# In the first two groups ScalarE also makes the lower part of R, eight more scaled copies of tri a tile

## The chip, the cores and the metric

The kernel runs on 1 core of a Trainium2 chip. Its time is device microseconds, the median over runs. TensorE (PE in the rows) multiplies matrices, VectorE (DVE) and ScalarE (ACT) work elementwise, GpSimd (POOL) does some small things, and SyncE (SP) issues the transfers.

## The reference, cut to what matters

A Mamba-2 mixer with a residual and a layer norm, then a gated feed-forward layer on 4-bit weights, again with a residual and a layer norm. Input is (16, 256, 256). The change lies in the mixer's decay matrices inside a chunk:

```python
zxbcdt = u @ W_in                       # z, xBC, dt
xBC = silu(causal_conv4(xBC) + conv_b)  # x, B, C
dt = softplus(dt + dt_bias); A = -exp(A_log)
dA = A * dt                             # one number per token and head (8 heads)
L = exp(segsum(dA))                     # decay from token s to token l
y_diag = einsum('bclhn,bcshn,bhcls,bcshp->bclhp', C, B, L, x * dt)
y = (y_diag + y_off + D * x) * silu(z); y = rmsnorm(y) * norm_scale
h = layernorm(u + y @ W_out)
out = layernorm(h + (gelu(h @ Wg.T) * (h @ Wu.T)) @ Wd.T)
```

## The kernel before

The work is cut into groups of tokens, in tiles of 128. Group -1 (`FIRST`) has two tiles, groups 0 to 6 have four, group 7 (`LAST`) has two. Each engine runs its own instruction stream, written out by hand, and semaphores join them. The names of the steps and their order are in `SLOTS`: for a group, the mixer's steps (x, z, CB, R, D, XT, Y, g, S, op, ln) stand between the sixteen units of the feed-forward layer of the group before it (gate, up, GELU, down). Group -1 has no group before it, so beside its mixer, and in group 0 beside both, stands the preparation of the weights: `decode`, `value` and `rest` on VectorE, `upper` and `lower` on ScalarE, the products of L655 and L657 on TensorE, placed by the tables `DECODE`, `VALUE`, `UPPER`, `TAKE_OFF` and `LOWER`. Groups 1 to 5 are one loop whose group number is a register; -1, 0, 6 and 7 are written out with a plain number.

Products in fp32 are made from operands that are split into an upper part, rounded to the matrix format, and a lower part, the rest. The same holds for dA. For each tile i the step R makes R[:, h, :] = tri * dA[:, i, h] for the 8 heads, in two parts: ScalarE makes the upper one with eight scaled copies (L728), VectorE the lower one with one multiplication on 128x1024 elements (L935). Group -1 writes them to the tile of hT (`R_first`), the others to the tile of uT. Step D on TensorE (L552, L553) waits for both parts (`R_h`, `R_l`) and multiplies them with `after_r` into two banks, which gives the sums of dA between two tokens. ScalarE takes the exponential of them into `dec` (L738; in tile 1 of group -1 into `act_sb`), VectorE multiplies them with the masked C B product `cb` (L953), and TensorE multiplies the result with xdt in step Y (L573, for odd tiles also L583). Then VectorE forms y (L965, L1002, L969), multiplies it with the gate z (L972), ScalarE squares it (L749) and rounds it to g_hi (L754), VectorE adds the squares (L976, L978) and makes g_lo (L980), TensorE multiplies with W_out, and VectorE adds to h_sb (L987). The layer norm ends in L1029, and the transposes of F1 (L626) start the feed-forward layer.

On ScalarE a unit is in_hi (L760) and the GELU (L774), on VectorE in_lo (L1035) and the gated product (L1049), which frees the up bank. The exponentials and the GELU use different tables of ScalarE, so a table load stands at each change between them in the groups that have both.

`wait_R` holds R of tile i until the E or D bank before it was read, since R has one buffer for all tiles.

Of the kernel before, what the change touches and what calls it, by code (L numbers as in the profile page):

```python
# [6 lines left out]
ACT = mybir.ActivationFunctionType  # L7
# [63 lines left out]
def kind_of(g):  # L71

    return {FIRST: "first", LAST: "last"}.get(g, "full") if isinstance(g, int) else "full"


def tiles(g):

    return 4 if kind_of(g) == "full" else 2
# [13 lines left out]
def split_name(name):  # L92

    number = "".join(c for c in name if c.isdigit())
    return name.replace(number, "") if number else name, int(number or 0)
# [15 lines left out]
def wait(eng, signal, group, k):  # L111

    value = signal.at(group, k)
    if not isinstance(value, int) or value > 0:
        eng.wait_ge(signal.sem, value)


def mamba_ffn_kernel(nc, u, u_t, W_in, channels, dt_bias, A_log, W_out, ffn_w, ffn_s, out):
    BATCH, SEQ, DM = u.shape
    DI = W_out.shape[0]  # L120
    H = dt_bias.shape[0]
# [34 lines left out]
    def width(g):  # L156
        return P * tiles(g)
# [3 lines left out]
    with ExitStack() as ctx:  # L161
        def sb(name, shape, dt=F32):
            return ctx.enter_context(nc.sbuf_tensor(name, shape, dt))

        def sig(name, per, first=None, step=1):
            return Signal(ctx.enter_context(nc.semaphore(name)), per, first, step)
# [10 lines left out]
        tri = sb("tri", [P, P])  # L177
# [19 lines left out]
        dA_hi, dA_lo = sb("dA_hi", [P, NT, H], F32R), sb("dA_lo", [P, NT, H], F32R)  # L197
# [28 lines left out]
        def R_of(g):  # L226
            return R_first if kind_of(g) == "first" else (R_hi, R_lo)

        def dec_of(g, i):
            return dec_first if kind_of(g) == "first" and i else dec  # L230
# [41 lines left out]
        R_h, R_l, dec_ok, W_ok = sig("R_hi_done", 4, 2), sig("R_lo_done", 4, 2), sig("decay_ready", 8, 4), sig("W_ready", 4, 2)  # L272
# [20 lines left out]
        def bank(g, use):  # L293
            return MB[USES[kind_of(g)].index(use) % 4]
# [6 lines left out]
        def wait_ready(eng, use, g):  # L301
            if isinstance(g, int) and g < FIRST:
                return
            s, k = ready(g, use)
            wait(eng, s, g, k)
# [25 lines left out]
        def wait_R(eng, i, g):  # L331

            if i:
                wait_ready(eng, f"D{i - 1}b" if i % 2 else f"E{i // 2 - 1}", g)
            elif kind_of(g) != "first":
                wait_ready(eng, "z3", g)
            wait(eng, dA_ok, g, 1)

        def f32(ap):
            return ap.bitcast(F32)  # L340

        def by_block(ap):
            return ap.rearrange("p (j l) -> p j l", j=JT)

        def tile_of(x, i):

            return x[:, 0:JT, i * P:(i + 1) * P]
# [331 lines left out]
        def _(act):  # L679
            def tanh(n, g):  # L680
                c = CONV_ORDER[n]
                wait(act, conv, g, 3 * n + 3)

                wait_ready(act, f"S{tiles(g - 1) - 1}", g - 1)
                if n >= 2:
                    wait(act, xbc_ok, g, n - 1)
                nc.scalar.activation(y[:, n % 2, 0:width(g)], xbc[:, c, 0:width(g)], ACT.Tanh).then_inc(x_tanh.sem, 1)

            def mixer(name, g):
                kind, i = split_name(name)  # L690
                if kind == "uT":

                    wait_ready(act, f"E{tiles(g - 1) // 2 - 1}", g - 1)
                    wait(act, uT_in, g, 1)
                    for k in range(KT):
                        nc.scalar.activation(uT_hi[:, k, 0:width(g)], u32[:, k, 0:width(g)], ACT.Copy)\
                            .then_inc(uT_h.sem, 1)
                elif kind == "x":
                    n = CONV_ORDER.index(i)
                    wait_ready(act, f"x{i}", g)  # L700

                    wait(act, y_step, g - 1, D_ADDED[tiles(g - 1) - 1])
                    nc.scalar.activation(xbc[:, i, 0:width(g)], bank(g, f"x{i}")[:, 0:width(g)], ACT.Identity,  # L703
                                         bias=chan[:, 24 + i:25 + i],
                                         scale=chan[:, 18 + i:19 + i]).then_inc(conv0.sem, 1)
                    if n == 0:
                        wait(act, dt_step, g, 3)
                        nc.scalar.activation(dte[:, 0:H * tiles(g)], dte[:, 0:H * tiles(g)], ACT.Exp).then_inc(dt_exp.sem, 1)
                    for m in (() if n < 2 else (0, 1) if n == 2 else (n - 1,)):
                        tanh(m, g)  # L710
                elif kind == "z":
                    if i == 3:
                        tanh(CT - 1, g)
                    wait_ready(act, f"z{i}", g)
                    wait(act, g_l, g - 1, tiles(g - 1))
                    nc.scalar.activation(zs[:, i, 0:width(g)], bank(g, f"z{i}")[:, 0:width(g)], ACT.Tanh, scale=0.5)\
                        .then_inc(z_tanh.sem, 1)
                elif kind == "CB":
                    wait_ready(act, f"CB{i}", g)
                    if i:  # L720
                        wait_ready(act, "Yoff0", g)
                    else:
                        wait_ready(act, f"Yoff{tiles(g - 1) // 2 - 1}", g - 1)
                    nc.scalar.activation(cb[:, 1, :], bank(g, f"CB{i}")[:, P:2 * P], ACT.Copy).then_inc(cb_act.sem, 1)
                elif kind == "R":
                    wait_R(act, i, g)
                    for h in range(H):
                        ins = nc.scalar.activation(R_of(g)[0][:, h, :], tri[:, :], ACT.Copy,  # L728
                                                   scale=f32(dA_hi[:, i, h:h + 1]))
                    ins.then_inc(R_h.sem, 1)  # L730
                elif kind == "D":
                    if i == 0:
                        wait_ready(act, f"Y{tiles(g - 1) - 1}", g - 1)
                    elif kind_of(g) != "first":
                        wait_ready(act, f"Y{i - 1}", g)
                    for n, use in enumerate((f"D{i}a", f"D{i}b")):
                        wait_ready(act, use, g)
                        nc.scalar.activation(dec_of(g, i)[:, 4 * n:4 * n + 4, :],  # L738
                                             bank(g, use)[:, :].rearrange("p (h l) -> p h l", h=4),
                                             ACT.Exp).then_inc(dec_ok.sem, 1)  # L740
                    if i % 2:

                        if i > 2:
                            wait_ready(act, f"S{i - 2}", g)
                        wait_ready(act, f"E{i // 2}", g)
                        nc.scalar.activation(y[:, 1, :], bank(g, f"E{i // 2}")[:, :], ACT.Exp).then_inc(e_ok.sem, 1)
                elif kind == "g":
                    wait(act, y_step, g, Y_DONE[i])
                    nc.scalar.activation(by_block(y[:, i % 2, :]), tile_of(zs, i), ACT.Square).then_inc(squared.sem, 1)  # L749
                    if i:  # L750
                        wait_ready(act, f"op{i - 1}", g)
                    else:
                        wait_ready(act, f"op{tiles(g - 1) - 1}", g - 1)
                    nc.scalar.activation(g_hi[:, :, :], tile_of(zs, i), ACT.Copy).then_inc(g_h.sem, 1)  # L754
# [53 lines left out]
            act.wait_ge(consts.sem, 5)  # L808
            nc.scalar.activation(minus_i, ident[:, :], ACT.Copy, scale=-1.0).then_inc(crt.sem, 1)
            mixer("uT", FIRST)  # L810
            act.wait_ge(bc_in.sem, 16)
            nc.scalar.activation(win_hi[:, :, B0:DT0], bc_raw[:, :, 0:DT0 - B0], ACT.Copy).then_inc(win_top.sem, 1)
# [15 lines left out]
        def _(dve):  # L828
# [62 lines left out]
            def mixer(name, g):  # L891
                kind, i = split_name(name)
# [3 lines left out]
                elif kind == "x":  # L896
# [5 lines left out]
                    for d in (1, 2, 3):  # L902
                        c = (3 - d) * CT + i
                        ins = stt(acc[:, :, d:], src[:, :, 0:SEQ - d], chan[:, c:c + 1], acc[:, :, d:],  # L904
                                  ALU.mult, ALU.add)
# [22 lines left out]
                elif kind == "CB":  # L928
# [1 line left out]
                    wait(dve, cb_act, g, i + 1)  # L930
                    tt(cb[:, 0, :], bank(g, f"CB{i}")[:, 0:P], tri[:, :], ALU.mult)
                    tt(cb[:, 2, :], bank(g, f"CB{i}")[:, 2 * P:3 * P], tri[:, :], ALU.mult).then_inc(cb_ok.sem, 1)
                elif kind == "R":
                    wait_R(dve, i, g)
                    tt(R_of(g)[1], tri[:, :].unsqueeze(1).to_broadcast([P, H, P]),  # L935
                       f32(dA_lo[:, i, :]).unsqueeze(2).to_broadcast([P, H, P]), ALU.mult).then_inc(R_l.sem, 1)
# [312 lines left out]
```

## Time and profile before

| | |
|---|---|
| median of 3 runs | 955.6 us (955.42 to 955.68) |
| profiled execution | 955.01 us, span 953.3 us |
| TensorE busy | 892.7 us (94%) |
| VectorE busy | 704.9 us (74%) |
| ScalarE busy | 532.2 us (56%) |
| mean granted TensorE clock | 0.971 of full speed |
| group -1 | up to about 75 us |
| group 0's mixer | about 75 to 178 us |

The span is the time from the first to the last instruction of the profiled execution. In a timeline each row is an operation: start, duration, engine, line, what it writes and reads, and in brackets for how long the engine had been idle before it and whose result released it. "issue" in the place of a releaser means that the profile shows none. Several operations of one line in a row are merged, as x8. Durations of neighbours can overlap a little, since an operation starts before the one ahead has fully ended.

### The profile page before, as it was taken

The numbers are of one execution on the slowest core, as the hardware profiler recorded it, in microseconds if no ns is written. First come the engines' busy times: TensorE is split into PE (matmuls) and PEld (weight loads), VectorE is DVE, ScalarE is ACT, GpSimd is POOL, SyncE is SP. The second block draws the span as 40 slices with busy tenths as digits, with TensorE's granted clock in tenths as the row PEclk, the third lists the DMA queues.
The fourth block names the chain that finished last, engine by engine and source line by source line (L and its number), as shares of the span: only waits on it lengthen the run. The fifth ranks groups of instructions, "written<-read, shape, count | busy, mean of one in ns | idle before, by whom it ended". The sixth has DMA issues, their size and how long they took to land.

```text
span 953.3 us, 16507 instructions
## 1 busy us (share of the span) xinstructions
PE 892.7 (94%) x5632; PEld 773.0 (81%) x5632; DVE 704.9 (74%) x1566; ACT 532.2 (56%) x1016; POOL 72.3 (8%) x104
## 2 busy tenths in 40 slices
PE   4777789899999999999999999999999999999997
PEld 3446678788898888888888888888888888888887
DVE  6767988787769776786779876786779776867453
ACT  4743486448645775448735674547635674456232
POOL 2101000200011000200020000200020000200000
PEclk9787899999999999999999999999999999999999
DMA  4111100010002000010001000010002000100010
GB/s 135 33 58 49 32 18 12 23 45 1 1 23 67 0 0 22 22 44 0 0 22 66 0 0 22 31 35 0 0 22 67 1 1 13 45 12 1 1 35 12
DMA packets 18651, 23.13 MB, mean 24 GB/s; under 512 B 1584, under 2 KB 15152, under 8 KB 18608
## 3 DMA queue, kind: packets, MB, share of 16 engines
q1 hardware_dynamic: 18176, 22.56, 7.4%
q8 instruction: 24, 0.39, 0.2%
q14 instruction: 19, 0.16, 0.1%
q10 hardware_dynamic: 432, 0.03, 0.0%
HBM read 14.19 MB, written 4.19 MB: 19 GB/s over the span
## 4 chain that ended last, share of the span: by engine, by line
PE 78%; DVE 10%; issue 6%; POOL 3%; ACT 2%; DMA 1%; POOLq 0%; DVEq 0%; SPq 0%; ACTq 0%
PE gate_bank L493 6%; PE up_bank L493 6%; PE up_bank L495 6%; PE up_bank L494 6%; PE gate_bank L495 5%; PE gate_bank L494 5%; PE down L493 5%; PE down L495 5%; PE mixer L493 5%; PE down L494 5%; PE mixer L495 5%; PE mixer L494 5%; PE mixer L573 3%; DVE xbc L904 2%; PE mixer L552 2%
## 5 line engine op out<-in xcount | busy, mean ns | idle before, releaser
L493 PE MATMUL down<-wd_hi,in_hi 128*128 128x256 f32 x512 | 145.1, 283 | 0.7 <-DVE in_lo L1035 0.7
L495 PE MATMUL down<-wd_hi,in_lo 128*128 128x256 f32 x512 | 144.0, 281 | 0.0
L494 PE MATMUL down<-wd_lo,in_hi 128*128 128x256 f32 x512 | 143.8, 281 | 0.0
L904 DVE SCALAR_TENSOR_TENSOR xbc<-mixer,chan,xbc 128x510 f32<-128x510 f32 (+1 forms) x162 | 110.9, 685 | 27.8 <-ACT xbc L703 26.1
L760 ACT ACTIVATE in_hi<-act_sb 128x512 fp32r<-128x512 f32 (+1 forms) x144 | 83.4, 579 | 65.3 <-PE down L495 53.7
L1049 DVE SCALAR_TENSOR_TENSOR act_sb<-up_bank,act_sb 128x512 f32<-128x512 f32 (+1 forms) x144 | 90.4, 628 | 37.5 <-PE up_bank L495 18.5
L774 ACT ACTIVATE act_sb<-gate_bank 128x512 f32<-128x512 f32 (+1 forms) x144 | 79.0, 548 | 67.7 <-PE gate_bank L495 67.0
L493 PE MATMUL gate_bank<-hT_hi,wg_hi 128*128 128x512 f32 (+1 forms) x288 | 111.4, 387 | 3.1 <-DVE wg_lo L1102 3.1
L493 PE MATMUL up_bank<-hT_hi,wu_hi 128*128 128x512 f32 (+1 forms) x288 | 108.4, 376 | 6.4 <-DVE act_sb L1049 6.4
L495 PE MATMUL up_bank<-hT_hi,wu_lo 128*128 128x512 f32 (+1 forms) x288 | 107.8, 374 | 0.0
L494 PE MATMUL up_bank<-hT_lo,wu_hi 128*128 128x512 f32 (+1 forms) x288 | 107.8, 374 | 0.0
L495 PE MATMUL gate_bank<-hT_hi,wg_lo 128*128 128x512 f32 (+1 forms) x288 | 107.1, 372 | 0.0
L494 PE MATMUL gate_bank<-hT_lo,wg_hi 128*128 128x512 f32 (+1 forms) x288 | 107.0, 371 | 0.0
L1035 DVE TENSOR_TENSOR in_lo<-act_sb,in_hi 128x512 fp32r<-128x512 f32 (+1 forms) x144 | 90.0, 625 | 20.7 <-ACT in_hi L760 20.7
L493 PEld LDWEIGHTS down<-wd_hi,in_hi 128*128 128x128 f32 x512 | 97.3, 190 | 5.6 <-DVE in_lo L1035 1.1
L494 PEld LDWEIGHTS down<-wd_lo,in_hi 128*128 128x128 f32 x512 | 97.2, 190 | 4.5
L703 ACT ACTIVATE xbc<-mixer,chan 128x512 f32<-128x512 f32 (+1 forms) x54 | 39.4, 729 | 107.2 <-PE mixer L495 107.2
L495 PEld LDWEIGHTS down<-wd_hi,in_lo 128*128 128x128 f32 x512 | 97.1, 190 | 0.0
L493 PE MATMUL mixer<-uT_hi,win_hi 128*128 128x512 f32 (+1 forms) x180 | 71.2, 395 | 12.4 <-DVE wdt L1126 11.4
L1159 POOL TENSOR_TENSOR rms<-rms_v,minus_half 128x1 f32<-128x1 f32 x32 | 20.1, 628 | 741.4 <-DVE rms_v L991 741.4
L728 ACT ACTIVATE uT_hi<-tri,dA_hi 128x128 fp32r<-128x128 f32 x240 | 73.2, 391 | 0.0
L493 PEld LDWEIGHTS up_bank<-hT_hi,wu_hi 128*128 128x128 f32 x288 | 55.2, 192 | 18.3 <-DVE act_sb L1049 8.0
(200 smaller groups left out, 1936.2 us busy)
## 6 DMA issues: line engine op xcount, KB each, us to landing
xbc<-in_u_t_dram SPq DMA_DIRECT2D x7, 512.0 KB, 3.6
h_sb<-in_u_dram SPq DMA_DIRECT2D x7, 512.0 KB, 3.8
h_res<-h_sb SPq DMA_DIRECT2D x7, 512.0 KB, 2.9
out_dram<-h_res SPq DMA_DIRECT2D x7, 512.0 KB, 2.9
scales<-in_ffn_s_dram SPq DMA_DIRECT2D x24, 128.0 KB, 2.1
packed<-in_ffn_w_dram SPq DMA_DIRECT2D x8, 96.0 KB, 2.1
xbc<-in_u_t_dram SPq DMA_DIRECT2D x2, 256.0 KB, 2.8
xbc<-in_W_in_dram SPq DMA_DIRECT2D x1, 512.0 KB, 6.2
```

The source lines that it names most:

```text
L493: nc.tensor.matmul(dst, lh, rh, start=first, stop=False, skip_group_check=True)
L494: nc.tensor.matmul(dst, lh, rl, start=False, stop=False, skip_group_check=True)
L495: return nc.tensor.matmul(dst, ll, rh, start=False, stop=last, skip_group_check=True)
L573: mm = nc.tensor.matmul(bank(g, use)[a * HP:(a + 1) * HP, j * P:(j + 1) * P], xdt[:, h * HP:(h + 1) * HP], dec_of(g, i)[:, h, :], start=Tr ...
L703: nc.scalar.activation(xbc[:, i, 0:width(g)], bank(g, f"x{i}")[:, 0:width(g)], ACT.Identity, bias=chan[:, 24 + i:25 + i], scale=chan[:, 18 ...
L728: ins = nc.scalar.activation(R_of(g)[0][:, h, :], tri[:, :], ACT.Copy, scale=f32(dA_hi[:, i, h:h + 1]))
L760: nc.scalar.activation(in_hi[:, n % 2, 0:width(f)], act_sb[:, n % 2, 0:width(f)], ACT.Copy)\
L774: nc.scalar.activation(act_sb[:, n % 2, 0:width(f)], GB[:, 0:width(f)], ACT.Gelu_apprx_tanh, scale=CODE_SCALE).then_inc(gelu_ok.sem, 1)
L904: ins = stt(acc[:, :, d:], src[:, :, 0:SEQ - d], chan[:, c:c + 1], acc[:, :, d:], ALU.mult, ALU.add)
L1035: tt(in_lo[at], act_sb[at], f32(in_hi[at]), ALU.subtract)\
L1049: stt(inter, UB[:, 0:width(f)], CODE_SCALE, inter, ALU.mult, ALU.mult)\
L1159: tt(rms[:, i:i + 1], rms_v[:, i:i + 1], half[:, 0:1], ALU.pow).then_inc(rms_ok.sem, 1)
```

## The change

A test on the group's number is added. Where it holds (groups -1 and 0, in all six tiles), ScalarE makes the lower part of R too, right behind the upper one, and VectorE leaves it out, with its wait. In the loop the number is a register and the test is false.

```diff
+        def lower_by_scalar(g):
+            return isinstance(g, int) and g <= 0
...
                     ins.then_inc(R_h.sem, 1)
+                    if lower_by_scalar(g):
+                        for h in range(H):
+                            ins = nc.scalar.activation(R_of(g)[1][:, h, :], tri[:, :], ACT.Copy,
+                                                       scale=f32(dA_lo[:, i, h:h + 1]))
+                        ins.then_inc(R_l.sem, 1)
...
-                elif kind == "R":
+                elif kind == "R" and not lower_by_scalar(g):
                     wait_R(dve, i, g)
                     tt(R_of(g)[1], tri[:, :].unsqueeze(1).to_broadcast([P, H, P]),
                        f32(dA_lo[:, i, :]).unsqueeze(2).to_broadcast([P, H, P]), ALU.mult).then_inc(R_l.sem, 1)
```

ScalarE's sequence in group -1, from R0 to the exponentials of D1, first before the change (lines are numbered as in each program; the changed one is 4 to 9 lines longer there):

```order
L728 ACTIVATE hT_hi<-tri,dA_hi 128x128 [waits dA_split]
L728 ACTIVATE hT_hi<-tri,dA_hi 128x128 x7
L738 ACTIVATE dec<-mixer 128x512 [waits mixer0_ready]
L738 ACTIVATE dec<-mixer 128x512 [waits mixer1_ready]
L728 ACTIVATE hT_hi<-tri,dA_hi 128x128 [waits dA_split,mixer1_ready]
L728 ACTIVATE hT_hi<-tri,dA_hi 128x128 x7
L738 ACTIVATE act_sb<-mixer 128x512 [waits mixer3_ready]
```

And the same place after it:

```order
L732 ACTIVATE hT_hi<-tri,dA_hi 128x128 [waits dA_split]
L732 ACTIVATE hT_hi<-tri,dA_hi 128x128 x7
L737 ACTIVATE hT_lo<-tri,dA_lo 128x128 x8
L747 ACTIVATE dec<-mixer 128x512 [waits mixer0_ready]
L747 ACTIVATE dec<-mixer 128x512 [waits mixer1_ready]
L732 ACTIVATE hT_hi<-tri,dA_hi 128x128 [waits dA_split,mixer1_ready]
L732 ACTIVATE hT_hi<-tri,dA_hi 128x128 x7
L737 ACTIVATE hT_lo<-tri,dA_lo 128x128 x8
L747 ACTIVATE act_sb<-mixer 128x512 [waits mixer3_ready]
```

Eight operations without a wait of their own now stand between each R and the exponentials behind it. The place on VectorE that gives up the lower parts of both tiles, before:

```order
L932 TENSOR_TENSOR cb<-mixer,tri 128x128
L935 TENSOR_TENSOR hT_lo<-tri,dA_lo 128x1024 [waits dA_split]
L948 COPY tail<-dec 128x8 [waits decay_ready]
L953 TENSOR_TENSOR dec<-dec,cb 128x1024 [waits cb_ready,tail_ready]
L1094 TENSOR_TENSOR h_res<-codes,scales 128x512 [waits weights_rest_in_bank,scales_in0,codes_ready]
L935 TENSOR_TENSOR hT_lo<-tri,dA_lo 128x1024 [waits dA_split,mixer1_ready]
L940 TENSOR_TENSOR xdt<-mixer,dt_sb 128x512 [waits mixer2_ready]
```

After:

```order
L941 TENSOR_TENSOR cb<-mixer,tri 128x128
L957 COPY tail<-dec 128x8 [waits decay_ready]
L962 TENSOR_TENSOR dec<-dec,cb 128x1024 [waits cb_ready,tail_ready]
L1103 TENSOR_TENSOR h_res<-codes,scales 128x512 [waits weights_rest_in_bank,scales_in0,codes_ready]
L949 TENSOR_TENSOR xdt<-mixer,dt_sb 128x512 [waits mixer2_ready]
```

The two multiplications and their waits are gone; what stood behind them moves up by one.

In group 0, ScalarE around R2 and R3, before (here stand the squares, g_hi and a unit behind R):

```order
L728 ACTIVATE uT_hi<-tri,dA_hi 128x128 x7
L724 ACTIVATE cb<-mixer 128x128 [waits mixer1_ready,mixer2_ready]
L749 ACTIVATE y<-zs 128x512 [waits y_step]
L754 ACTIVATE g_hi<-zs 128x512 [waits mixer1_ready]
L760 ACTIVATE in_hi<-act_sb 128x256 [waits down_done,inter_ready]
L774 ACTIVATE act_sb<-gate_bank 128x256 [waits inter_lo,gate_ready]
```

And after:

```order
L732 ACTIVATE uT_hi<-tri,dA_hi 128x128 x7
L737 ACTIVATE uT_lo<-tri,dA_lo 128x128 x8
L728 ACTIVATE cb<-mixer 128x128 [waits mixer1_ready,mixer2_ready]
L758 ACTIVATE y<-zs 128x512 [waits y_step]
L763 ACTIVATE g_hi<-zs 128x512 [waits mixer1_ready]
L769 ACTIVATE in_hi<-act_sb 128x256 [waits down_done,inter_ready]
L783 ACTIVATE act_sb<-gate_bank 128x256 [waits inter_lo,gate_ready]
```

The eight stand ahead of cb, the square, g_hi and the unit's two operations; nothing else is in another place, and TensorE's sequence is the same as before.

## Rows read from the trace of the kernel before

**Rows 1.** the page, part 1: busy us of the span by engine (share), instructions.

```profile
PE 892.7 (94%) x5632; PEld 773.0 (81%) x5632; DVE 704.9 (74%) x1566; ACT 532.2 (56%) x1016; POOL 72.3 (8%) x104
```

**Rows 2.** stretches: start:end, length, busy PE PEld DVE ACT POOL, clock, DMA share, GB/s.

```profile
40.00:45.00 5.00, 4.90 (x11) 3.04 (x11) 2.17 (x4) 3.43 (x11) 0.00 (x0) 0.53 0.02 3
46.00:55.00 9.00, 8.03 (x67) 5.57 (x68) 7.32 (x17) 5.37 (x11) 0.00 (x0) 1.00 0.18 50
115.00:145.00 30.00, 24.33 (x175) 21.48 (x176) 26.75 (x55) 24.35 (x55) 0.00 (x0) 0.89 0.06 19
145.00:178.00 33.00, 27.42 (x227) 25.53 (x225) 26.07 (x64) 17.43 (x37) 6.29 (x8) 0.95 0.05 17
200.00:300.00 100.00, 99.81 (x641) 86.71 (x641) 74.10 (x161) 59.92 (x110) 8.09 (x10) 1.00 0.04 13
300.00:900.00 600.00, 597.26 (x3769) 518.00 (x3767) 448.77 (x977) 345.99 (x641) 42.01 (x54) 1.00 0.06 18
```

**Rows 3.** timeline, ScalarE, group -1: start, duration, operation, [idle before <-releaser].

```profile
37.57 2.43 ACT L728 ACTIVATE hT_hi<-tri,dA_hi 128x128 fp32r<-128x128 f32 x8
...
42.66 2.44 ACT L728 ACTIVATE hT_hi<-tri,dA_hi 128x128 fp32r<-128x128 f32 x8
46.81 1.09 ACT L738 ACTIVATE act_sb<-mixer 128x512 f32<-128x512 f32 x2 [1.72 <-PE mixer L553]
```

**Rows 4.** timeline, VectorE, group -1.

```profile
42.79 0.17 DVE L948 COPY tail<-dec 128x8 f32<-128x8 f32 x1 [3.74 <-ACT dec L738]
...
44.74 1.22 DVE L935 TENSOR_TENSOR hT_lo<-tri,dA_lo 128x1024 fp32r<-128x1024 f32 x1
...
49.23 1.22 DVE L953 TENSOR_TENSOR act_sb<-act_sb,cb 128x1024 f32<-128x1024 f32 x1
...
54.91 0.69 DVE L965 TENSOR_TENSOR y<-mixer,y 128x512 f32<-128x512 f32 x1 [1.51 <-PE mixer L583]
```

**Rows 5.** timeline, TensorE, group -1.

```profile
40.05 0.79 PE L552 MATMUL mixer<-hT_hi,after_r 128*128 128x512 f32 x1 [4.27 <-ACT hT_hi L728]
...
46.06 0.47 PE L552 MATMUL mixer<-hT_hi,after_r 128*128 128x512 f32 x1 [1.10 <-ACT hT_hi L728]
...
52.91 1.09 PE L573 MATMUL mixer<-act_sb,xdt 128*64 128x128 f32 x16 [0.91 <-issue]
```

**Rows 6.** timeline, ScalarE, group 0.

```profile
125.89 2.44 ACT L728 ACTIVATE uT_hi<-tri,dA_hi 128x128 fp32r<-128x128 f32 x8
...
132.22 0.63 ACT L781 ACTIVATE wu_hi<-h_res 128x512 fp32r<-128x512 f32 x1 [2.48 <-DVE h_res L1094]
...
138.15 2.44 ACT L728 ACTIVATE uT_hi<-tri,dA_hi 128x128 fp32r<-128x128 f32 x8
...
140.65 0.62 ACT L749 ACTIVATE y<-zs 128x512 f32<-128x512 f32 x1
...
148.72 2.44 ACT L728 ACTIVATE uT_hi<-tri,dA_hi 128x128 fp32r<-128x128 f32 x8
151.06 0.62 ACT L749 ACTIVATE y<-zs 128x512 f32<-128x512 f32 x1
```

**Rows 7.** timeline, VectorE, group 0.

```profile
143.46 0.41 DVE L976 TENSOR_TENSOR y<-y 128x256 f32<-128x256 f32 x1
...
151.86 0.41 DVE L976 TENSOR_TENSOR y<-y 128x256 f32<-128x256 f32 x1
...
155.81 0.42 DVE L1049 SCALAR_TENSOR_TENSOR act_sb<-up_bank,act_sb 128x256 f32<-128x256 f32 x1
...
162.75 0.68 DVE L965 TENSOR_TENSOR y<-mixer,y 128x512 f32<-128x512 f32 x1
```

**Rows 8.** timeline, TensorE, group 0.

```profile
157.72 0.28 PE L493 MATMUL up_bank<-hT_hi,wu_hi 128*128 128x256 f32 x1
...
160.65 1.09 PE L573 MATMUL mixer<-dec,xdt 128*64 128x128 f32 x16
...
178.12 1.13 PE L626 MATMUL gate_bank<-ident,h_sb 128*128 128x128 f32 x4 [3.56 <-DVE h_sb L1029]
```

## The prediction, as put on record before the changed kernel was run

> **What bounds the kernel now.** I read the page first: TensorE is busy 94% of the span, VectorE 74%, ScalarE 56% [rows 1]. Shares of a whole span say little about two groups out of nine, so the table of stretches comes next [rows 2]. From 200 us on TensorE works without a gap (99.81 of 100 us, 597.26 of 600 us): no later stretch has a reserve in which a delay could vanish, and the change doesn't touch those groups either. Up to 178 us it is different. Between 115 and 178 us TensorE is busy 51.75 of 63 us, and waits for the other two: VectorE is busy 26.75 of 30 us from 115 to 145 us, ScalarE 24.35. So in the part that the change touches both engines are nearly full, and the question is which of them a step waits for. For that I read the timelines of the three engines, first for group -1 [rows 3 to 5], then for group 0 [rows 6 to 8], and looked in each at the idle time ahead of a row and its releaser.
>
> **The change part by part.** For six tiles (R0, R1 of group -1, R0 to R3 of group 0) VectorE loses one operation on 128x1024 elements, and ScalarE gets eight more on 128x128. The VectorE one takes 1.22 us [rows 4]. Eight ScalarE ones take 2.44 us, and the operation behind them starts 2.34 us after the first (148.72 to 151.06) [rows 6]. The new eight have the same form and a scale of the same kind, so I take 2.34 us for them too. VectorE is relieved of 6 x 1.2 = 7.2 us, ScalarE is given 6 x 2.34 = 14.0 us. TensorE's D step needs both parts, and they were made side by side; now they are made one after the other. Nothing else is moved: no DMA, no GpSimd instruction, and no other order on any engine.
>
> **Group -1.** ScalarE starts R0 at 37.57 us [rows 3], and TensorE, idle for 4.27 us, starts D0 at 40.05, when the eighth is done [rows 5]. VectorE then has nothing to do for 3.74 us, until the exponentials of D0 [rows 4]. So the whole 2.34 us goes on the path, and taking R0's lower part from VectorE gives nothing. R1 starts at 42.66 [rows 3], right behind the exponentials of D0, so it too is 2.34 us later, at 45.00, and its sixteen end at 45.00 + 2 x 2.34 + 0.1 = 49.8 us. D1 started at 46.06 [rows 5]; the name in the row is ScalarE's, but ScalarE's part ended at 45.10, and the last thing that D1 needed was VectorE's lower part (44.74 + 1.22 = 45.96 [rows 4]). So the wait that is removed there was a real one, worth 0.9 us, and the new one is longer: D1 goes from 46.1 to 49.8 us, +3.8. TensorE's work behind it is in one piece up to Y1, where it had to wait 0.91 us for VectorE's xdt [rows 5]. VectorE comes only some 2.5 us later now: its product of tile 1 stood at 49.23 [rows 4] though the exponentials of D1 were done at 46.81 + 1.09 = 47.90 [rows 3]; they are now done near 51.7, and it starts then. That difference of 1.3 us covers TensorE's wait, which is used up, and Y1 starts +2.9 us later, near 55.8. VectorE's next step waits for TensorE directly (54.91, 1.51 us idle [rows 4]), so it moves by the same 2.9, and from there to the start of group 0 one chain of dependent steps (y, squares, output product, norm, transposes) carries it on. Bounds: 2.3, were all of R1 hidden, and 3.8, were nothing absorbed. I take **+2.9 us**.
>
> **Group 0**, in times relative to this group's new start. R0 pushes ScalarE back by 2.34 us: the GELU, the table load and the exponentials behind it. VectorE's product waits for them, TensorE for that, so R1 (125.89 [rows 6]) starts 2.34 us later and ends 4.68 us later. Behind it ScalarE waited 2.48 us for VectorE's weights (132.22 [rows 6]); VectorE, free of two lower parts, has those weights early enough, so this wait is used up: 4.68 - 2.48 = +2.2. R2 (138.15) starts 2.2 later and ends 4.54 later. The square behind it ended at 140.65 + 0.62 = 141.27 [rows 6], VectorE asked for it at 143.46 [rows 7]: a reserve of 2.15, leaving +2.4 on VectorE and on everything that waits for it, ScalarE's next operation among it. R3 (148.72) starts at +2.4, ends at +4.7. Here there is next to no reserve: the square ended at 151.68, VectorE used it at 151.86 [rows 6, 7]. VectorE moves by 4.5 us, and with it the gated product of the unit (155.81 becomes 160.3, done at 160.7 [rows 7]). TensorE's product into that bank stood at 157.72 and must now wait for it: +3.0 [rows 8]. The down and output products and Y3 (160.65) stand behind it on TensorE without a gap [rows 8]; VectorE's step at 162.75, which uses their result, moves with it [rows 7]. From there the chain to the transposes at 178.12 is again VectorE and TensorE in turn; TensorE stands idle for 3.56 us at its end [rows 8], so nothing there absorbs it. **+3.0 us**. Bounds: 0, if ScalarE's idle time took all of it, and 4.5, if R3's whole delay stayed.
>
> Of VectorE's 7.2 us nearly nothing comes back, because behind each removed operation it meets a ScalarE result that is later than before. Sum: 2.9 + 3.0 = 5.9 us. The profiled execution took 955.01 us (span 953.3, 1.7 around it); with 5.9 it is 960.9. The median of the runs is 0.6 above that execution, 955.6, which gives **961.5 us**.
>
> **TensorE's clock** is the unknown. From 40 to 45 us, after its idle time, the granted clock was 0.53 (mostly the 1.2 GHz level), from 46 to 55 us 1.00 (2.4 GHz) [rows 2]; a D matmul that starts at 40.05 lasts 0.79 us, one at 46.06 lasts 0.47 [rows 5]. Ahead of D1 TensorE will now idle some 2.5 us instead of 1.10. If the clock stays low for D1 and what follows up to Y1, that is up to half of 8.03 us of busy time [rows 2], of which a part hides behind VectorE: 0 to +3 us. The other way, a stretch at the low level elsewhere (the mean was 0.89 from 115 to 145 us) can fall on idle time instead: -1.5 us.
>
> **The rivals.**
> 1. *Faster: VectorE is the bound.* It is the fuller engine of the two, 26.75 of 30 us, and ScalarE is the one with spare time: 5.7 us from 115 to 145, 15.6 us from 145 to 178 [rows 2]. If those figures decided, 7.2 us would come off: 948.4 us. It decides as soon as VectorE's queue, and not a result of ScalarE, is what D, Y and the squares wait for. The one place where that is so is R1 of group -1, 0.9 us, and there the new work costs more. Chance 0.05. The Trainium skill (Perfetto Trace Analysis, Optimizing Scalar/DVE Operations) says that offloading to ScalarE may make sense where VectorE is saturated; by that rule this rival would be the forecast. The rows with idle time ahead of D0 and ahead of VectorE speak against it here. The same skill (ScalarE: Activation LUTs, Rules for kernel authors) advises VectorE for a plain multiplication; the rows agree, 2.34 against 1.2 us a tile.
> 2. *Hidden in group 0.* ScalarE's idle time there, 21.2 us, is more than the 9.4 us it is given. Were the places right, only group -1 would pay: 955.6 + 2.9 = 958.5 us. Against it stand the square at 151.06 with 0.18 us to spare and the exponentials right behind each R. Chance 0.10.
> 3. *No change*, both groups absorbed: it needs D0 of group -1 not to wait for ScalarE, and it waits. 955.6 us, chance 0.03.
> 4. *The clock goes against it too:* 961.5 + 2.5 = 964.0 us. Chance 0.13.
> That the change doesn't do what it says can be left out: its test on the group's number is settled when the program is built, and the sequences show six more groups of eight on ScalarE and six fewer operations on VectorE.
>
> **How the numbers follow.** Forecast 0.69; slower by more than 0.2% (957.5 us or more, about what a measurement of this kernel can tell from no change) holds the forecast, rivals 2 and 4: 0.69 + 0.10 + 0.13, less 0.03 for the low end of rival 2 with a kinder clock = 0.89. Within 0.2%: 0.06. Faster: 0.05. The range goes from rival 2 with some help from the clock, 957.7, to the forecast with all 3 us of the clock, 964.5.
>
> **What would show it.** Right: the sixteen operations on ScalarE in one piece of 4.7 us a tile; D0 of group -1 near 42.4 us and D1 near 49.8; VectorE idle ahead of more rows up to 178 us, with ScalarE as releaser; transposes of F1 near 77.3 and 184.0 us (before 74.4 and 178.1); the same 99.8% busy TensorE after that. Wrong: if the second set of eight takes much less or more than 2.34 us; if the R rows of group 0 start where they did but the transposes at its end don't move (rival 2); if D1 is not late (rival 1); or if the granted clock between 50 and 60 us is near 0.5 (rival 4).

## The result, and the profile after

The changed kernel took **965.5 us** in the median (963.4 to 967.6 in four runs), beside 955.5 us for the kernel before: ratio 1.0103, interval 1.0084 to 1.0122. It is slower, as forecast, but by 10.0 us and not by 5.9, and so lies 1.0 us above the range (957.7 to 964.5). The profiled execution took 965.75 us, with a span of 964.0 us, 10.7 more than before. Each ratio below is against the kernel before as it was timed beside that run (955.5 or 955.6 us).

The changed kernel's page, part 1: busy us, share of the span and instructions of each engine.

```profile
PE 895.9 (93%) x5632; PEld 775.9 (80%) x5632; DVE 698.9 (73%) x1560; ACT 546.4 (57%) x1064; POOL 73.2 (8%) x104
```

Against [rows 1] VectorE lost six operations and 6.0 us, ScalarE gained 48 operations and 14.2 us (forecast: 7.2 and 14.0). The work moved as said; what it cost is a question of places. Stretches of the changed kernel (start:end, length, busy time of PE, PEld, DVE, ACT, POOL, granted clock, DMA share, GB/s):

```profile
40.00:45.00 5.00, 2.04 (x5) 1.69 (x6) 0.00 (x0) 3.46 (x11) 0.00 (x0) 0.50 0.00 0
46.00:58.00 12.00, 8.82 (x38) 5.77 (x37) 7.95 (x16) 8.00 (x22) 0.00 (x0) 0.70 0.11 31
...
300.00:900.00 600.00, 597.24 (x3759) 517.74 (x3759) 452.70 (x989) 351.84 (x648) 41.96 (x54) 1.00 0.06 20
```

And the same stretch of the kernel before, for the second of them:

```profile
46.00:58.00 12.00, 9.20 (x69) 5.87 (x69) 10.21 (x23) 5.96 (x11) 0.00 (x0) 1.00 0.14 39
```

The steady part is what it was (597.24 of 600 us, [rows 2]). From 46 to 58 us TensorE is busy nearly as long as before, but with 38 instead of 69 instructions, at a granted clock of 0.70 instead of 1.00. The timelines say where. ScalarE, group -1, changed kernel (start, duration, operation, [idle time before <-releaser]):

```profile
38.10 2.43 ACT L732 ACTIVATE hT_hi<-tri,dA_hi 128x128 fp32r<-128x128 f32 x8
40.43 2.43 ACT L737 ACTIVATE hT_lo<-tri,dA_lo 128x128 fp32r<-128x128 f32 x8
...
45.53 2.43 ACT L732 ACTIVATE hT_hi<-tri,dA_hi 128x128 fp32r<-128x128 f32 x8
47.87 2.43 ACT L737 ACTIVATE hT_lo<-tri,dA_lo 128x128 fp32r<-128x128 f32 x8
```

TensorE of the same: D0, the last product ahead of the wait for D1 (L545), D1, Y0, Y1 and the transposes F1 that end the group.

```profile
42.96 0.76 PE L556 MATMUL mixer<-hT_hi,after_r 128*128 128x512 f32 x1 [6.48 <-issue]
...
46.62 0.60 PE L545 MATMUL mixer<-ident,xbc 128*128 128x128 f32 x4
50.40 0.77 PE L556 MATMUL mixer<-hT_hi,after_r 128*128 128x512 f32 x1 [3.18 <-issue]
50.97 0.63 PE L557 MATMUL mixer<-hT_lo,after_r 128*128 128x512 f32 x1
...
54.09 1.98 PE L577 MATMUL mixer<-dec,xdt 128*64 128x128 f32 x16
...
59.05 1.09 PE L577 MATMUL mixer<-act_sb,xdt 128*64 128x128 f32 x16
...
79.85 0.50 PE L630 MATMUL gate_bank<-ident,h_sb 128*128 128x128 f32 x2 [4.13 <-DVE h_sb L1038]
```

Both sets of eight take 2.33 to 2.34 us from start to start. D1 moves from 46.06 [rows 5] to 50.40, Y1 from 52.91 to 59.05, F1 from 74.41 to 79.85. And D1 itself is another thing than before: its first matmul lasts 0.77 us instead of 0.47, the next 0.63, and the sixteen of Y0 take 1.98 us, where those of Y1, at the same form, take 1.09. The four products of L545 just ahead of the wait take 0.60 us, as they do in the kernel before at full clock, so the clock had come up before the wait of 3.18 us and was low behind it.

In group 0, at its last tile, ScalarE, then VectorE (the addition of the squares of tiles 2 and 3, and y of tile 3), then TensorE (D0 of the group, the second half of D3, E of tile 3, F1, and the first product of the next group), all of the changed kernel:

```profile
156.80 2.44 ACT L732 ACTIVATE uT_hi<-tri,dA_hi 128x128 fp32r<-128x128 f32 x8
159.14 2.44 ACT L737 ACTIVATE uT_lo<-tri,dA_lo 128x128 fp32r<-128x128 f32 x8
161.48 0.62 ACT L758 ACTIVATE y<-zs 128x512 f32<-128x512 f32 x1
```

```profile
151.45 0.43 DVE L985 TENSOR_TENSOR y<-y 128x256 f32<-128x256 f32 x1
...
162.14 0.43 DVE L985 TENSOR_TENSOR y<-y 128x256 f32<-128x256 f32 x1 [2.19 <-ACT y L758]
...
172.59 0.69 DVE L974 TENSOR_TENSOR y<-mixer,y 128x512 f32<-128x512 f32 x1 [0.17 <-PE mixer L587]
```

```profile
128.19 0.76 PE L556 MATMUL mixer<-uT_hi,after_r 128*128 128x512 f32 x1 [2.53 <-issue]
...
164.57 0.50 PE L556 MATMUL mixer<-uT_hi,after_r 128*128 128x512 f32 x1 [0.62 <-DVE y L1011]
...
165.90 0.49 PE L566 MATMUL mixer<-uT_hi,tri_r 128*128 128x512 f32 x1 [0.59 <-DVE xdt L949]
...
187.94 1.13 PE L630 MATMUL gate_bank<-ident,h_sb 128*128 128x128 f32 x4 [3.56 <-DVE h_sb L1038]
...
191.00 0.63 PE L497 MATMUL mixer<-uT_hi,win_hi 128*128 128x512 f32 x1
```

VectorE waits 2.19 us for the square, as foreseen. TensorE, which passed D3 and E without a wait before, now waits in two places that the prediction did not name: 0.62 us for VectorE's L1011, 0.59 us for its L949.

**The ledger.** Each line is the shift of one start against the kernel before, in the two profiled executions; "new here" is what came on since the line above, and the last column what the forecast had for that.

| place | before | after | shift | new here | forecast |
|---|---|---|---|---|---|
| R0 of group -1 | 37.57 | 38.10 | 0.53 | 0.53, ahead of every changed instruction | 0 |
| D1 | 46.06 | 50.40 | 4.34 | 3.81 | 3.8 |
| Y1 | 52.91 | 59.05 | 6.14 | 1.80 | -0.9 |
| F1 of group -1 | 74.41 | 79.85 | 5.44 | -0.70 | 0 |
| first product of group 0's mixer (L545) | 115.58 | 121.36 | 5.78 | 0.34 | 0 |
| F1 of group 0 | 178.12 | 187.94 | 9.82 | 4.04 | 3.0 |
| end of the span | 953.3 | 964.0 | 10.7 | 0.9 | 0 |

### The profile page after: what moved, and what is told of

Read it like the earlier page. It is cut to its first block, busy times and chain, and to the rows that moved or that the text cites. A ratio compares the mean times of both kernels' runs of the same rounds, so it can differ in the third digit from the quotient of the medians.

```text
span 964.0 us, 16544 instructions
## 1 busy us (share of the span) xinstructions
PE 895.9 (93%) x5632; PEld 775.9 (80%) x5632; DVE 698.9 (73%) x1560; ACT 546.4 (57%) x1064; POOL 73.2 (8%) x104
## 4 chain that ended last, share of the span: by engine, by line
PE 79%; DVE 8%; issue 6%; ACT 4%; POOL 2%; DMA 1%; POOLq 0%; DVEq 0%; SPq 0%; ACTq 0%
PE gate_bank L497 6%; PE up_bank L497 6%; PE up_bank L499 6%; PE up_bank L498 6%; PE gate_bank L498 5%; PE gate_bank L499 5%; PE mixer L497 5%; PE down L497 5%; PE down L499 5%; PE down L498 5%; PE mixer L499 5%; PE mixer L498 5%; PE mixer L577 3%; PE mixer L556 2%; PE mixer L566 2%
## 5 line engine op out<-in xcount | busy, mean ns | idle before, releaser
L1058 DVE SCALAR_TENSOR_TENSOR act_sb<-up_bank,act_sb 128x512 f32<-128x512 f32 (+1 forms) x144 | 90.3, 627 | 38.1 <-PE up_bank L499 19.5
L497 PE MATMUL mixer<-uT_hi,win_hi 128*128 128x512 f32 (+1 forms) x180 | 72.0, 400 | 12.7 <-DVE wdt L1135 11.7
L499 PE MATMUL mixer<-uT_hi,win_lo 128*128 128x512 f32 (+1 forms) x180 | 69.4, 385 | 0.0
```

The lines of the kernel that those rows point to most:

```text
L497: nc.tensor.matmul(dst, lh, rh, start=first, stop=False, skip_group_check=True)
L499: return nc.tensor.matmul(dst, ll, rh, start=False, stop=last, skip_group_check=True)
L1058: stt(inter, UB[:, 0:width(f)], CODE_SCALE, inter, ALU.mult, ALU.mult)\
```

## The experiments

The first four tell the groups and the clock apart, the next four the tiles of group 0 and the other groups; the last two look for a faster kernel.

**Group -1 alone.**

```
-            return isinstance(g, int) and g <= 0
+            return isinstance(g, int) and g == FIRST
```

> The change in group -1 alone (two tiles). Theory, waits and clock: R0 is fully on the path, R1 partly, 2.9 us, and TensorE, idle longer ahead of D1, runs D1 and what follows at 1.2 GHz, 2.0 us more: about 960.4 us (958.4 to 961.5), more than half of the whole loss from a third of the tiles. Rival, the cost goes by ScalarE's added work, 10.0 us over six equal tiles: 955.5 + 3.3 = 958.8 us.

Measured: 961.4 us, ratio 1.0065 (1.0044 to 1.0085), +5.7 us on a prediction of 2.9. The cost by added work would have been 3.3 us; the interval starts at 4.2. So about half of the loss comes from the two tiles of group -1, a third of the added work. D1 starts at 50.28, after 2.81 us of idle time, and its first matmul lasts 0.71 us: the low clock comes back in a second kernel. Here it ends with the eight matmuls of D1 and E (Y0 takes 1.09 us again), so that Y1 starts at 57.70, 7.42 us behind D1, where it was 8.65 in the changed kernel. From the start of R0 to F1 group -1 takes 41.25 us, against 36.84 before and 41.75 in the changed kernel: +4.4 and +4.9.

**Group 0 alone.**

```
-            return isinstance(g, int) and g <= 0
+            return isinstance(g, int) and g == 0
```

> The change in group 0 alone (four tiles). Theory, waits and clock: R0 to R3 cost 4.0 us in group 0, with 0 to 1 us for the clock: about 959.5 us (959 to 961). Rival, cost by added work: 955.5 + 6.7 = 962.2 us.

Measured: 960.8 us, ratio 1.0059 (1.0041 to 1.0077), +5.1 us. The interval (3.9 to 7.4 us) holds the expected 4.0 and the rival's 6.7 alike, so the places decide. From F1 to F1 it takes 182.64 - 74.47 = 108.17 us, where the kernel before took 103.71: +4.5. But 0.7 of it lies between F1 and the group's first product (L545), where nothing was changed: 41.84 us, as in seven other kernels (41.83 or 41.84), where the profiled execution of the kernel before had 41.17. From that first product to E of tile 3 it takes 44.28 us instead of 40.50: **+3.8**, not 3.0. 5.7 and 5.1 make 10.8, beside 10.0 of the whole change: within what the runs can tell the two groups add, and neither hides the other. The two bank waits of tile 3 are there as well (TensorE, group 0 alone):

```profile
159.26 0.51 PE L556 MATMUL mixer<-uT_hi,after_r 128*128 128x512 f32 x1 [0.61 <-DVE y L1011]
...
160.59 0.50 PE L566 MATMUL mixer<-uT_hi,tri_r 128*128 128x512 f32 x1 [0.60 <-DVE xdt L949]
```

**The changed kernel with TensorE kept at work ahead of D0 and D1.** 13 and 7 matmuls whose result D overwrites fill part of TensorE's idle time in group -1; the rest is the changed kernel.

```
                 elif kind == "D":
+                    if kind_of(g) == "first":
+                        wait_bank(pe, f"D{i}a", g)
+                        for _ in range((13, 7)[i]):
+                            nc.tensor.matmul(bank(g, f"D{i}a")[:, :], after_r[:, :],
+                                             win_hi[:, 0, 0:512], start=True, stop=True)
```

> The changed kernel, with extra matmuls on TensorE (13 ahead of D0, 7 ahead of D1 in group -1; 128x512 into the bank that D then overwrites) in the time in which it was idle there. Nothing else changes. Theory: the granted clock ahead of D1 no longer falls, D1 to Y0 run at 2.4 GHz and Y1 of group -1 comes about 2 us earlier: 963.5 us, and D1's first matmul lasts 0.47 us instead of 0.77. Rival, the low clock only falls on time in which TensorE waits anyway: unchanged, 965.5 us, although the matmuls are shorter.

Measured: 963.8 us, ratio 1.0091 (1.0066 to 1.0115). Its TensorE (D0, D1, Y1, F1), and its stretch from 46 to 58 us:

```profile
42.43 0.77 PE L561 MATMUL mixer<-hT_hi,after_r 128*128 128x512 f32 x1 [3.62 <-issue]
...
49.88 0.47 PE L561 MATMUL mixer<-hT_hi,after_r 128*128 128x512 f32 x1 [1.68 <-issue]
...
55.74 1.09 PE L582 MATMUL mixer<-act_sb,xdt 128*64 128x128 f32 x16
...
76.27 0.70 PE L635 MATMUL gate_bank<-ident,h_sb 128*128 128x128 f32 x2 [4.13 <-DVE h_sb L1043]
```

```profile
46.00:58.00 12.00, 10.32 (x79) 7.20 (x78) 8.87 (x19) 9.45 (x24) 0.00 (x0) 1.00 0.14 41
```

The totals don't decide: the interval (961.9 to 966.6 us) holds both the expected 963.5 and the rival's 965.5. The places do. D1 starts where it started in the changed kernel (49.88; 50.40 less the offset of 0.53 is 49.87), but at 0.47 us a matmul, and Y1 starts at 55.74: **+2.83 us** against before, where the prediction had +2.9. D0, ahead of which 3.62 us of idle time were left, still runs at the low level. So the working of group -1 up to Y1 was right for a full clock at D1, and what was missing is the clock: Y1 was 2.78 us later without these matmuls (58.52 without the offset), and F1 3.05 us (79.32 and 76.27). About 1.7 us of it is left at F1 of group 0 and between the two medians, since group 0 took 109.46 us here instead of 108.09 from F1 to F1: its last E began at the low clock too (0.80 us for the first matmul; 0.49 in the changed kernel).

**The kernel before with the same** (13 and 4 matmuls).

> The kernel before, with 13 extra matmuls ahead of D0 and 4 ahead of D1 in group -1, as a control. Theory: D0 then runs at 2.4 GHz, its four matmuls take 1 us instead of 1.7 and the weights' products behind it are shorter too; D1 waits for VectorE, so at most 0.5 to 1 us comes off: 954.5 to 955.5 us. Rival: no change, or slower by the 0.3 us by which the extra ones can run over: 955.8 us.

Measured: 954.2 us, ratio 0.9995 (0.9982 to 1.0008). D0 and D1 run at full clock (0.50 and 0.47 us), Y1 starts at 51.86 instead of 52.91, of which 0.2 is an earlier R0. A local gain of 0.8 us; the total doesn't tell it from nothing. Before the change, then, the idle time ahead of D0 cost little; after it the idle time ahead of D1 cost more, because D1, E and Y0 stand behind it in one piece.

**One tile of group 0 at a time.** Here the test takes the tile too; the three kernels differ in the number.

```
-                    if lower_by_scalar(g):
+                    if lower_by_scalar(g, i):
...
-            return isinstance(g, int) and g <= 0
+            return isinstance(g, int) and g == 0 and i == 1
```

Tile 1 alone:

> The change for one tile alone, R1 of group 0. Theory, waits: behind this R ScalarE waited 2.48 us for VectorE's weights, which now come 1.1 us earlier, since VectorE is rid of the lower part ahead of them; so ScalarE's exponentials of D1 and VectorE's product come at the same time or up to 0.3 us earlier: 955.4 us (955.2 to 955.8), and the transposes at the end of group 0 stay within 0.4 us of their place. Rival, cost by added work (9.9 us over six tiles): 955.5 + 1.65 = 957.2 us.

Tile 3 alone:

> The change for one tile alone, R3 of group 0. Theory, waits: ScalarE's square has 0.2 us of reserve, so VectorE's sums move by 2.2 us and the step on x and the product xdt behind them too; TensorE's second D matmul pair and its E matmuls write banks that these two steps read, and wait for them: E starts 1.7 us later than before. 955.5 + 1.7 = 957.2 us (956.7 to 957.9). With tile 1 at zero and this at 1.7, the tiles are not alike. Rival, no wait for banks: only the up bank decides, 0.7 us: 956.2 us. The clock's phase can move either by 1 us, so the places in the trace decide: E matmuls of tile 3 against the start of group 0.

Tile 0 alone:

> The change for one tile alone, R0 of group 0. Theory, waits: ScalarE's whole 2.34 us lie ahead of the exponentials of D0, VectorE's product waits for them, and VectorE is without a gap from there to R3, so nothing takes it back: 955.5 + 2.3 = 957.8 us, and the transposes at the end of group 0 stand 2.3 us later against its start. With tile 1 at -0.4 and tile 3 at +1.7. Rival, equal tiles: +1.65 us, or, if tile 0's delay is taken up by VectorE's idle time of 0.8 us ahead of that product, 957.0 us.

| tile of group 0 | time | ratio (interval) | F1 to F1, against 103.71 | first product of the group to E of tile 3, against 40.50 |
|---|---|---|---|---|
| 0 | 958.2 | 1.0023 (1.0011 to 1.0035) | 106.13, +2.4 | 42.23, +1.7 |
| 1 | 954.2 | 0.9987 (0.9978 to 0.9997) | 103.28, -0.4 | 39.38, -1.1 |
| 3 | 958.5 | 1.0021 (1.0008 to 1.0035) | 106.16, +2.4 | 42.26, +1.8 |

The last column is the one to go by: in all three kernels 0.7 us of the column before it lies ahead of the group's first product, where nothing was changed (41.83 or 41.84 us from F1, as above). It also agrees with the totals (+2.2, -1.2 and +2.0 us by the ratios), of which tile 1 came out below its expected range and tile 3 above. The same eight operations cost 1.7 us in tile 0 and gain 1.1 in tile 1. A price per tile doesn't exist; the place makes it. In tile 1 ScalarE had 2.48 us of idle time behind R [rows 6]. With the eight in it the row is (ScalarE, tile 1 alone)

```profile
133.23 0.64 ACT L790 ACTIVATE wu_hi<-h_res 128x512 fp32r<-128x512 f32 x1
```

with no idle time ahead of it, and VectorE's 1.2 us are free. In tile 3 (TensorE, tile 3 alone) both bank waits stand without any other tile's delay:

```profile
157.24 0.51 PE L556 MATMUL mixer<-uT_hi,after_r 128*128 128x512 f32 x1 [0.62 <-DVE y L1011]
...
158.57 0.49 PE L566 MATMUL mixer<-uT_hi,tri_r 128*128 128x512 f32 x1 [0.59 <-DVE xdt L949]
```

Counted from Y0 of the group, E starts 1.75 us later than before, which is what the banks alone would make; the other 0.7 us of the 2.4 lie ahead of Y0. The wait of 0.59 us ahead of E is there with tile 0 alone as well, and even with tile 1 alone, where E comes earlier than before: it shows what TensorE waits for, and the place of E shows what that costs.

These three kernels leave group -1 as it was, and still say something about its clock. In those for tiles 0 and 1 R0 starts at 37.91 and 37.94, and D1 runs at the low clock behind a wait of only 0.95 us (TensorE, tile 1 alone):

```profile
44.43 1.05 PE L545 MATMUL mixer<-ident,xbc 128*128 128x128 f32 x4
46.44 0.76 PE L556 MATMUL mixer<-hT_hi,after_r 128*128 128x512 f32 x1 [0.95 <-ACT hT_hi L732]
```

In the kernel for tile 3 R0 starts at 37.62, and D1, behind the same 0.95 us, takes 0.47 us. So the unchanged code has D1 at either level. The products of L545 differ from those of the changed kernel: 1.05 us instead of 0.60, that is, the clock had not come up yet after the wait ahead of D0. The low D1 costs 0.5 to 0.6 us here (7.35 and 7.41 us from D1 to Y1 instead of 6.85), since it runs on the wait of 0.91 us ahead of Y1; in the kernel for group -1 alone, where that wait is used up, the same eight slow matmuls cost 1.6 us (7.42 instead of 5.86).

**All groups.**

```
-            return isinstance(g, int) and g <= 0
+            return True
```

> The change in all groups, 30 tiles instead of 6. Theory, waits: in the later groups TensorE has its own work in line (99.8% busy) and D starts 1.8 us after R's upper part is done, so 2.34 us more of ScalarE are mostly hidden, 0 to 0.5 us a tile: 965.5 to 975 us, and TensorE at 98% or more from 210 us on. Rival, ScalarE's added work costs the same everywhere (1.65 us a tile): 965.5 + 40 = 1005 us.

Measured: 974.7 us, ratio 1.0199 (1.0175 to 1.0222), 9.2 us over the changed kernel for the other 26 tiles (208 more instructions on ScalarE), 0.35 us a tile; the kernel has 32 tiles, not the 30 of the expectation. Its stretch, to be read against the one of the changed kernel above:

```profile
300.00:900.00 600.00, 592.77 (x3717) 512.36 (x3716) 424.47 (x958) 397.83 (x820) 41.26 (x53) 1.00 0.06 20
```

ScalarE is given 46 us here and VectorE loses 28, and TensorE loses 4.5 of its 600. Where TensorE has work queued the move is nearly hidden, and it still brings nothing: TensorE loses time although VectorE has 28 us less to do.

**VectorE helps ScalarE with R0 of group -1.** The opposite of the change: VectorE makes the upper part of two heads, ScalarE of six.

```
-                    for h in range(H):
+                    for h in range(H - 2 if kind_of(g) == "first" and i == 0 else H):
...
+                    if kind_of(g) == "first" and i == 0:
+                        tt(R_of(g)[0][:, H - 2:, :], tri[:, :].unsqueeze(1).to_broadcast([P, 2, P]),
+                           f32(dA_hi[:, i, H - 2:]).unsqueeze(2).to_broadcast([P, 2, P]), ALU.mult)
```

> The opposite of the change, at its dearest place: the kernel before, but in R0 of group -1 VectorE also makes the upper part of two heads (128x256, ahead of the lower part), ScalarE six instead of eight. Theory: D0 waits for ScalarE there, so it starts 0.58 us earlier (39.5 instead of 40.05), less if VectorE's two operations become the last: 955.5 - 0.5 = 955.0 us. Rival, VectorE is what the first group waits for: 955.5 + 0.4 = 955.9 us, D0 no earlier.

Measured: 954.4 us, ratio 0.9994 (0.9980 to 1.0007). From the start of R0 to D0 it takes 1.92 us instead of 2.48, as expected; the total can't be told from no change.

**The three together**, on the kernel before: the extra matmuls (13 and 4), the two heads, and the lower part of tile 1 of group 0 on ScalarE.

> The kernel before with the three things that helped or should help at their places: the extra matmuls ahead of D0 and D1 of group -1 (13 and 4), two heads of R0's upper part on VectorE, and the lower part of R1 of group 0 on ScalarE. Theory: 0.8, 0.6 and 0.4 us add up, since they lie on one chain: 955.5 - 1.8 = 953.7 us, at the edge of what the runs can tell. Rival, they hide one another and the clock's phase evens them out: 955.5 us.

Measured: **952.8 us**, ratio 0.9978 (0.9966 to 0.9990), 0.22% faster than the kernel before and 12.7 us below the changed one by the medians. Its D0 and D1 (TensorE):

```profile
39.29 0.49 PE L561 MATMUL mixer<-hT_hi,after_r 128*128 128x512 f32 x1 [0.68 <-ACT hT_hi L737]
...
44.45 0.47 PE L561 MATMUL mixer<-hT_hi,after_r 128*128 128x512 f32 x1 [1.51 <-ACT hT_hi L737]
```

Three gains, of which only one (tile 1, 0.13%) stood out of the noise alone, are clear in sum.

## Why the prediction was half right

**Right, by its own steps.** That VectorE, the fuller engine, is not what the steps wait for: rival 1 (faster) and rival 3 (no change) are out, and so is rival 2, since group 0 alone costs 5.1 us. The eight operations at 2.34 us. Group -1 up to D1, +3.8 forecast and 3.81 measured; up to Y1 at full clock, +2.9 and 2.83 (the third experiment). In group 0, counted from its first product (which stands 5.78 us later): VectorE at the addition of the squares of tile 2 at 151.45 instead of 143.46, +2.2 for the forecast +2.4 (the reserve of that square was 2.19 us, not 2.15), and of tile 3 at 162.14 instead of 151.86, +4.5 for +4.5. The idle time of 2.48 us in tile 1 is used up, and 99.8% busy TensorE follows from 200 us on.

**Wrong: the clock, taken at nothing.** The prediction put a price of 0 to +3 us on TensorE's clock after a longer wait for D1, called it the unknown, and took 0. In the trace D1 has 3.18 us of idle time ahead of it instead of 1.10, and runs at 0.63 us a 128x512 matmul where it ran at 0.39 to 0.40, which is the 1.2 GHz level against the 2.4 GHz one. From D1 to Y1 that is 8.65 us instead of 6.85, though the wait of 0.91 us ahead of Y1 is gone: 2.7 us of clock, which lies inside the 0 to +3 us of the prediction. Filling that idle time with matmuls gave Y1 2.78 us back, so the price is shown. From Y1 to F1 the changed kernel takes 20.80 us instead of 21.50, with a granted clock of 0.92 (59 to 80 us) instead of 0.84 (53 to 75 us), so by these two profiles **+2.0 us** stay. This gain of 0.7 us doesn't come from D1: with D1 at full clock it is 0.97 us (20.53, the filled kernel), and with D1 at the low clock in the kernel for group -1 alone there is none (21.52). By the sum's own terms group -1 was 4.9 and not 2.9, and 4.4 in the two other kernels with the change there and no extra matmuls (group -1 alone and all groups: 41.25 and 41.24 us from R0 to F1).

What lowers the clock is shown less firmly than what it costs. In all three kernels that have the longer wait and no extra matmuls (3.18, 2.81 and 2.86 us) the product ahead of it ran at or near the full clock and D1 behind it at the low one; with the wait cut to 1.68 us D1 ran at full clock. But this is one profiled execution of each kernel, the filled kernel's R0 came early (37.56) and that of the three late (37.95 to 38.10), and the unchanged group -1 can have a low D1 of its own where R0 comes late. A changed kernel with an early R0 and no extra matmuls was not seen. What the change certainly does is to take away the 0.91 us ahead of Y1 on which the unchanged kernel's low D1 could run.

Rival 4 had the mechanism and gave it a chance of 0.13; it even named the sign to look for, a low clock between 50 and 60 us (0.50 from 50 to 54 us, 0.67 over the ten). Two readings spoke for it in advance: D0 stood behind a wait of 4.27 us and ran at 0.79 us a matmul, D1 behind 1.10 us and ran at 0.47 [rows 5]. The forecast wait ahead of D1 was some 2.5 us, in the middle, and the price of the two ends was far from the same. With nothing to say which end was nearer, half of the 3 us was a better value than none.

Two more shifts stand in the ledger where no changed instruction is: 0.34 us between F1 of group -1 and the first product of group 0, and 0.9 us behind F1 of group 0, where the first 128x512 products last 0.63 us (191.00, above) and lasted 0.39 to 0.41 before. No later group has a reserve, so they reach the end. That they are a price of the change is not shown: the first stretch takes 40.96 to 41.84 us and the second 774.6 to 776.1 us among kernels that do the same there, and the kernel for group 0 alone, with the same four tiles, has 775.06 behind F1, where the kernel before has 775.18 and the changed one 776.06.

**Wrong: the bank that TensorE waits for in group 0.** The prediction followed the late VectorE to the up bank (157.72 before [rows 8]) and took the +3.0 us that TensorE would wait there. That this bank is free late was right, but ahead of it in TensorE's order stand the second half of D3 and E of tile 3, each of which takes a mixer bank that VectorE has to have read: D3's second bank after L1011 (y of tile 2), E's after L949 (xdt of tile 3). Both readers stand on VectorE behind the square that was late. TensorE waited 0.62 and 0.59 us for them in the changed kernel. When it came to the up bank, at 167.64, that bank had been free for 1.1 us (166.10 + 0.41, VectorE's L1058), so no wait was left there. E's shift is 9.82 us (156.08 to 165.90), and so is F1's (178.12 to 187.94): it is E's bank, and nothing behind it, that sets the end of the group. The term was 4.04 and not 3.0, and 3.8 in the kernel for group 0 alone. The tile-3 kernel shows the same two waits alone, and group 0 alone shows them too. What wasn't tried is to take away these two waits and leave the rest.

**The tiles of group 0.** The prediction had +2.2 us once R0 and R1 were made. In the changed kernel R2 starts at 145.96 instead of 138.15, +2.0 counted from the group's first product, so that step stands. The tiles alone don't add up to the whole: +1.7, -1.1 and +1.8 make 2.4 us of the 3.8 for group 0 alone. Tile 2 was not tried alone, and how the rest divides between it and what the tiles do to one another stays open.

**The rest.** 0.53 us of the 10.7 in the two profiles lie ahead of every changed instruction. They belong to the execution: kernels whose group -1 is that of the kernel before show R0 at 37.94 and 37.91 (tiles 1 and 0) as well as at 37.62 (tile 3), and the medians differ by 10.0 and not by 10.7. Why R0 comes at two such times stays open. The sum of the two profiles: 2.9 (group -1, work) + 2.0 (its clock) + 0.34 + 4.04 + 0.9 = 10.2 us, beside 10.0 between the medians. The agreement is in part luck, since the 0.34 and the 0.9 come and go from kernel to kernel.

The Trainium skill (Perfetto Trace Analysis, Optimizing Scalar/DVE Operations) says that offloading to ScalarE may make sense where VectorE is saturated. Here that holds for one of the three tiles of group 0 that were measured alone (tile 1, -0.13%), the one where the receiving engine had idle time at that very place.

## What to carry to other kernels

Price moved work place by place: what the receiving engine's next result has in reserve there, not how full the two engines are; the same eight operations cost 1.7 us in one tile and gained 1.1 in another. Where a delay gets through to an engine in order, walk its queue from the front and look at every bank that the delayed engine must have read, since a wait nearer the front can set the shift and leave nothing of the one that is easiest to see. And where a change lengthens TensorE's idle time ahead of a long piece, give the lower clock a value of its own, read from the rows at either level, and don't leave it at zero because it isn't known.

## What was not expected of the hardware

In group -1 the low clock behind the longer wait ahead of D1 cost up to Y1 nearly as much as the moved work itself (2.7 us beside 2.9): the eight matmuls of D1 and E came every 0.43 us instead of every 0.23, and the sixteen of Y0 took 1.98 us instead of 1.09. With a wait of 1.68 us (the changed kernel with extra matmuls) D1 ran at full clock. Matmuls that compute nothing of use, put into a bank that the next step overwrites, had filled the rest of it; of the 3.05 us that they brought up to F1, 1.4 us were lost again in group 0, whose own waits were not filled.

The length of the wait is not the whole of it: the same code of group -1, with the same 0.95 us ahead of D1, ran D1 at 0.47 us a matmul in one kernel and at 0.76 and 0.77 in two others, where all of group -1 stood 0.3 us later. So a single profile can show either level at one place, and a price of the clock has to be read from several.
